# A decoder layer on one core: first norm folded into the second, router by eight-largest, convolution as matmuls, new order on every engine

## The reference, cut to what matters

```python
x = layernorm(x + mamba(x))              # no learned scale, eps 1e-5
x = layernorm(x + retention(x, ctx))     # q from x, k and v from ctx
x = layernorm(x + moe(x))

# mamba: inner width 256, 16 states
x_b, z = split(x @ W_in)
xc    = silu(conv_b + sum_k shift(x_b, 3 - k) * conv_w[:, k])      # 4 taps, causal
delta = softplus((xc @ W_x)[:, :8] @ W_dt + b_dt);  B, C = (xc @ W_x)[:, 8:24], [:, 24:40]
h_t   = exp(delta * A) * h_{t-1} + delta * B * xc                   # 256 channels x 16 states
y     = (sum_s h * C + D * xc) * silu(z);  out = y @ W_out
# retention: q, k rotated; ((q k^T) * decay_mask) v, no softmax: linear in q
# moe: logits = x @ W_r + bias; top 2 of 16 experts (first index on ties), softmax of the two;
#      sum of the chosen experts down(silu(gate) * up), plus one shared expert
```

## Time and profile before

| | |
|---|---|
| time, median of three | 1213.99 us |
| the profiled execution: its own time, its span | 1216.39 us, 1214.6 us |
| first scan starts, last scan ends | 31.05 us, about 1137.6 us |
| busy in the span: VectorE, TensorE, ScalarE, GpSimd | 1093.3, 1080.0, 997.8, 989.8 us |
| ScalarE table loads | 163, 1283 ns each |
| TensorE's granted clock, mean | 0.967 |

### The profile page before, as it was taken

The page is one execution under the profiler, slowest core; times in us unless marked ns, Lnnn a source line. Parts: engine busy times, 40 slices in busy tenths (PEclk is TensorE's granted clock), DMA queues, the critical chain, the costliest instruction groups (busy, mean ns, idle before and its releaser), DMA issues.

```text
span 1214.6 us, 18948 instructions
## 1 busy us (share of the span) xinstructions
PE 1080.0 (89%) x6049; PEld 766.0 (63%) x6049; DVE 1093.3 (90%) x1598; ACT 997.8 (82%) x2288; POOL 989.8 (81%) x623
## 2 busy tenths in 40 slices
PE   5677888989999898999989898998989899988897
PEld 2455666666666766666666666666666667666565
DVE  2899999999999999999999999999999999999523
ACT  5677888989888898988889898988889898888343
POOL 0587797979988897998888799888979888898844
PEclk9687999999999999999999999999999999999999
DMA  6344454545464454546455444645444465454221
GB/s 181 141 164 154 142 174 150 187 141 182 158 202 158 159 183 143 188 150 209 150 169 173 159 173 153 206 160 173 159 172 161 157 204 165 159 179 158 70 80 58
DMA packets 84116, 194.55 MB, mean 160 GB/s; under 512 B 17288, under 2 KB 47936, under 8 KB 67632
## 3 DMA queue, kind: packets, MB, share of 16 engines
q1 hardware_dynamic: 84016, 193.33, 47.3%
HBM read 179.14 MB, written 5.77 MB: 152 GB/s over the span
## 4 chain that ended last, share of the span: by engine, by line
ACT 34%; DVE 26%; PE 24%; issue 11%; POOL 3%; DMA 0%; SPq 0%; DVEq 0%; POOLq 0%; ACTq 0%
ACT decay L680 15%; PE bank L283 14%; DVE state L822 14%; DVE drive_bank L720 6%; PE y_bank L287 6%; ACT L680 4%; ACT silu L656 2%; PE down_bank L283 2%; PE bank L287 2%; ACT L636 1%; ACT L648 1%; ACT L656 1%; POOL hid L916 1%; ACT x_rows L526 1%; POOL read L873 1%
## 5 line engine op out<-in xcount | busy, mean ns | idle before, releaser
L873 POOL TENSOR_TENSOR read<-state,bc_all 128x1024 f32<-128x1024 f32 x256 | 605.4, 2365 | 162.4 <-DVE state L822 139.0
L822 DVE TENSOR_TENSOR_SCAN state<-decay,drive_bank 128x512 f32<-128x512 f32 x512 | 593.9, 1200 | 0.0
L680 ACT ACTIVATE decay<-delta,a_neg 128x252 f32<-128x252 f32 x1024 | 420.4, 494 | 0.8
L720 DVE TENSOR_TENSOR drive_bank<-dx_bank,bc_all 128x512 f32<-128x512 f32 x512 | 327.3, 685 | 0.3 <-DVE state L822 0.3
L287 PE MATMUL y_bank<-ident,read 128*128 128x128 f32 x2048 | 285.7, 287 | 40.4 <-POOL read L873 40.3
L287 PEld LDWEIGHTS y_bank<-ident,read 128*128 128x128 f32 x2048 | 246.2, 148 | 90.6 <-POOL read L873 57.6
L916 POOL TENSOR_TENSOR hid<-gu,comb_all 128x512 f32<-128x512 f32 (+1 forms) x136 | 165.0, 1213 | 20.1 <-DVE gu L837 16.6
L283 PE MATMUL down_bank<-down_w,hid 128*128 128x128 f32 x1024 | 140.9, 280 | 15.1 <-POOL hid L916 12.6
L656 ACT ACTIVATE silu<-bank 128x512 f32<-128x512 f32 (+1 forms) x153 | 87.3, 571 | 81.4 <-PE bank L283 79.6
L283 PEld LDWEIGHTS down_bank<-down_w,hid 128*128 128x128 f32 x1024 | 127.0, 191 | 38.0 <-POOL hid L916 28.6
L837 DVE TENSOR_TENSOR gu<-silu,bank 128x512 f32<-128x512 f32 (+1 forms) x136 | 86.8, 638 | 56.7 <-PE bank L283 30.0
(11 more groups left out here) (126 smaller groups left out, 1496.3 us busy)
## 6 DMA issues: line engine op xcount, KB each, us to landing
bc_all<-bc_dram SPq DMA_DIRECT2D x128, 1024.0 KB, 4.9
comb_all<-comb_dram SPq DMA_DIRECT2D x240, 128.0 KB, 4.5
x_in<-in_x_dram SPq DMA_DIRECT2D x15, 256.0 KB, 6.0
ctx_in<-in_ctx_dram SPq DMA_DIRECT2D x15, 256.0 KB, 5.2
k_pair<-k_pair SPq DMA_DIRECT2D x30, 128.0 KB, 2.1
q_pair<-q_pair SPq DMA_DIRECT2D x30, 128.0 KB, 2.0
out_dram<-y_out SPq DMA_DIRECT2D x15, 256.0 KB, 5.6
comb_all<-comb_dram SPq DMA_DIRECT2D x32, 64.0 KB, 2.7
```

The source lines that it names most:

```text
L680: done = e.activation(seqs(decay_t[j % DECAYS][:, i, h, :])[:, :, 1:T], seqs(delta[c % 2][:, h, sub * SUB:(sub + 1) * SUB])[:, :, 1:T], AC ...
L720: e.tensor_tensor(drive_bank[:, n, :, :], dx_bank[:, :, :], bc_all[group % BC_BUFS][:, 0, PAIR * i + n, :].unsqueeze(1).to_broadcast([P, H ...
L822: e.tensor_tensor_scan(one(state_t[j % STATE_BUFS], n), one(decay_t[j % DECAYS], n), one(drive_bank, n), 0.0, ALU.mult, ALU.add).then_inc( ...
L873: e.tensor_tensor(read_t[j % READS][:, :, :, :], state_t[j % STATE_BUFS][:, :, :, :], bc_all[group % BC_BUFS][:, 1, PAIR * i:PAIR * (i + 1 ...
```

## The change

Slots give way to ticks, four to a step, and every stage is placed anew from one table, in ticks after the begin of its chunk, and once more for the last chunk. (The stages of each step keep their relations: drive and scan on VectorE, `read` at the fourth tick, the transposes two steps later.)

```diff
+TICKS, SUM_AFTER = 4, 2
+AT = {
+    "xT_mm": [(-45, -52)],  "tap_mm": [(-42, -40), (-36, -38)],  "proj_mm": [(-34, -28)],
+    "out_mm": [(69, 69)],  "x1T": [(68, 68)],  "r1_var_mm": [(85, 71)],  "r1_var": [(87, 74)],
+    "xc": [(-33, -42), (-31, -31)],  "top_tanh": [(131, 112)],
+    "dx": [(-12, -14), (10, -14)],  "dx_bank": [(-5, -9), (30, -83)],
+    "gate_mm": [
+        (136, 143), (139, 162), (142, 164), (151, 186), (156, 188), (163, 206), (176, 212), (179, 260), (179, 261)],
+    "gu": [
+        (140, 131), (142, 142), (148, 146), (156, 179), (164, 206), (173, 213), (180, 213), (187, 257), (189, 262)],
+    "pick": [(134, 114)],  "weigh": [(134, 120)],
...
+}
+WHOLE_DRIVES = (3, 7)
+WHOLE_SCANS = (3,)
+EXP_AT = [-10, -9, -4, -3, -3, 1, 3, 17, 21, 21, 28, 37, 37, 39, 41, 53]
-        EXP_AT = [10, 27]
-        EXP_SLOTS = 7
-        FFN_AT = [69, 70, 72, 76, 78, 84, 88, 90, 91]
```

```diff
-                if (c := chunk_at(slot, -21, -22)) is not None:
-                    mm(bank.t[:, 0:width(c)], w_in[:, P:2 * P], xT[c % 3][:, 0:width(c)]).then_inc(S["xb_mm"], 1)
+                for c, h in due(tick, "tap_mm"):
                     for n in range(TAPS):
+                        done = mm(seqs(bank.t[:, 0:width(c)])[:, :, n:T], w_tap[:, h, TAPS - 1 - n, :],
                                   seqs(xT[c % 3][:, 0:width(c)])[:, :, 0:T - n], start=n == 0, stop=n == TAPS - 1)
```

```diff
-                        mm(bank.t[:, cols], xT[c % 3][:, cols], center[:, :], stop=False)
-                        for h in range(HALVES):
-                            done = mm(bank.t[:, cols], y_gatedT[:, h, cols], w_out[:, h, :], start=False,
+                    mm(bank.t[:, 0:width(c)], center[:, :], xT[c % 3][:, 0:width(c)], stop=False)
+                    for h in range(HALVES):
+                        done = mm(bank.t[:, 0:width(c)], w_out[:, h, :], y_gatedT[:, h, 0:width(c)], start=False,
-                    square(bank_of["out", c][:, :], x1, LN1, c)
-                    normalise(bank_of["out", c][:, :], x1, LN1, c)
+                    copy(x1T[:, 0:width(c)], bank_of["out", c][:, 0:width(c)]).then_inc(S["x1T"], 1)
+                    e.activation(r1_sq[:, 0:width(c)], bank_of["out", c][:, 0:width(c)], ACT.Square, scale=D ** -0.5)
+                    for q in range(blocks_of(c)):
+                        done = mm(bank.t[:, 2 * q:2 * q + 2], r1_sq[:, q * P:(q + 1) * P], eps_col[:, :])
+                    e.activation(r1_var[:, 0:blocks_of(c)], of_block[:, :, 0], ACT.Copy, bias=LN_EPS * LN_EPS,
+                    e.tensor_tensor(var_eps[i][:, 0:n], squares[i][:, 0:n], r1_var[:, 0:n], ALU.add)
```

```diff
+                    for q in range(n):
+                        done = e.max(top[:, q, :], logits[:, q, :])
+                    e.tensor_tensor(rank[:, 0, 0:n, :], logits[:, 0:n, :], second, ALU.is_equal)
+                    e.tensor_tensor(soft[:, 0, 0:n], top[:, 0:n, 0], top[:, 0:n, 1], ALU.subtract)
+                    e.tensor_tensor(rank[:, 1, 0:n, :], rank[:, 0, 0:n, :], back..., ALU.mult)
+                    e.tensor_tensor(hot[:, 0, 0:n, :], logits[:, 0:n, :], second, ALU.is_gt)
+                    for q in range(n):
+                        done = e.max(top_at[:, q, :], rank[:, 1, q, :])
+                    e.tensor_scalar(soft[:, 4, 0:n], soft[:, 0, 0:n], 0.0, 0.5, ALU.is_equal, ALU.mult)
+                    e.tensor_tensor(hot[:, 1:3, 0:n, :], back..., top_at..., ALU.is_equal)
+                    e.tensor_tensor(weighted[:, :, 0:n, :], hot[:, :, 0:n, :], soft[:, 2:5, 0:n]..., ALU.mult)
+                    e.tensor_reduce(comb..., weighted..., AXIS.X, ALU.add)
+                    e.activation(soft[:, 1, 0:n], soft[:, 0, 0:n], ACT.Tanh, scale=0.5)          # ScalarE
+                    e.activation(soft[:, 2, 0:n], soft[:, 1, 0:n], ACT.Copy, bias=0.5, scale=0.5)
+                    e.activation(soft[:, 3, 0:n], soft[:, 1, 0:n], ACT.Copy, bias=0.5, scale=-0.5)
```

```diff
+                step = (j + SUB_STEPS) % (SUBS * SUB_STEPS)
+                if 0 <= j < STEPS and part < (1 if step in WHOLE_DRIVES else PAIR):
+                    a, b = (0, PAIR) if step in WHOLE_DRIVES else (part, part + 1)
+                if 0 <= j < STEPS and PAIR <= part < PAIR + (1 if step in WHOLE_SCANS else PAIR):
```

More of the change, by code:

```diff
@@ L236, in half_at @@
[L236 to L248, removed]
@@ new lines, in decoder_layer @@
+        DUE = {name: {} for name in AT}
+        for name, places in AT.items():
+            for n, (normal, last) in enumerate(places):
+                due_of(name, n, normal, last)
+        EXP_DUE = {}
+        for j in range(STEPS):
+            half, n = divmod(j, SUB_STEPS)
+            virtual, sub = divmod(half + 1, SUBS)
+            step = SUB_STEPS * sub + n
+            place = SUB_TICKS * (SUBS * virtual - 1) + (EXP_AT[step] if virtual < CHUNKS - 1 else LAST_EXP_AT[step])
+            EXP_DUE.setdefault(place, []).append(j)
@@ L277, in take @@
                     w.wait_ge(*bank.free)
-                bank.slot = slot + until
+                bank.slot = tick + until
                 bank_of[key] = bank.t
@@ L356, in _ @@
                     bank.free = (S["flip_copy"], 3)
-                if (c := chunk_at(slot, 31, 9)) is not None:
-                    bank = take(("ctxT", c), slot, 1)
+                for c in due(tick, "ctxT_mm"):
+                    bank = take(("ctxT", c), tick, 2)
                     w.wait_ge(S[f"ctx_load{c % 2}"], 16 * (c // 2 + 1))
@@ L364, in _ @@
                     bank.free = (S["ctxT"], at(c))
-                if (c := chunk_at(slot, 35, 35)) is not None:
-                    bank = take(("k", c), slot, 1)
+                for c in due(tick, "k_mm"):
+                    bank = take(("k", c), tick, 2)
                     w.wait_ge(S["ctxT"], at(c))
@@ L370, in _ @@
                     bank.free = (S["k_copy"], at(c))
-                if (c := chunk_at(slot, 36, 35)) is not None:
-                    bank = take(("v", c), slot, 1)
+                for c in due(tick, "v_mm"):
+                    bank = take(("v", c), tick, 2)
                     w.wait_ge(S["ctxT"], at(c))
@@ L413, in _ @@
+                for c in due(tick, "q_mm"):
+                    bank = take(("q", c), tick, 2)
                     w.wait_ge(S["x1T"], at(c))
@@ L425, in _ @@
                     bank.free = (S["ret_copy"], at(c))
-                if (c := chunk_at(slot, 54, 47)) is not None:
-                    bank = take(("retout", c), slot, 4.5)
+                for c in due(tick, "retout_mm"):
+                    bank = take(("retout", c), tick, 9)
                     w.wait_ge(S["ret"], at(c))
@@ L443, in _ @@
                     bank.free = (S["x2T"], at(c))
-                if (c := chunk_at(slot, 63, 56)) is not None:
-                    bank = take(("router", c), slot, 1.5)
+                for c in due(tick, "router_mm"):
+                    bank = take(("router", c), tick, 3)
                     w.wait_ge(S["x2T"], at(c))
@@ L643, in _ @@
-                for part, where in enumerate((4, 21, 17)):
-                    if (half := half_at(slot, where, part)) is not None:
-                        c, sub = half
-                        w.wait_ge(S["z_mm"], subs_before(c) + sub + 1)
-                        w.wait_ge(S["y_gated"], subs_before(c))
-                        e.activation(gate_z[:, sub, :, :].rearrange("p q n -> p (q n)"), bank_of["z", c, sub][:, :],
-                                     ACT.Silu, scale=1.0).then_inc(S["gate_z"], 1)
@@ L650, in _ @@
-                for index, (where, last) in enumerate(zip(FFN_AT, LAST_FFN_AT)):
-                    if (c := chunk_at(slot, where, last)) is None:
-                        continue
+                for c, sub in due(tick, "gate_z"):
+                    w.wait_ge(S["z_mm"], subs_before(c) + sub + 1)
+                    w.wait_ge(S["y_gated"], subs_before(c))
+                    e.activation(gate_z[:, sub, :, :].rearrange("p q n -> p (q n)"), bank_of["z", c, sub][:, :],
+                                 ACT.Silu, scale=1.0).then_inc(S["gate_z"], 1)
@@ L653, in _ @@
+                for c, index in due(tick, "silu"):
                     total = TILES * c + index
```

642 lines of the change are left out of this document (331 added, 311 removed).

## The result

The kernel after takes 1198.69 us (median of four runs, 1194.01 to 1204.63), beside 1214.42 for the kernel before in the same comparison (four runs, 1212.94 to 1217.0). The ratio is 0.987, with an interval of 0.982 to 0.992: faster by some 16 us (1.3%, which is clear of the noise but small), where 46 were forecast. The time is inside the range given, but only a third of the gain came.

The account below looks back on a forecast made before the run. VectorE was taken to bound the kernel, with TensorE leading after the change. A period 2.7 us shorter over 15.7 periods gave -42.4, with the tail -46.4: about 1168 us, range 1132 to 1204.

Parts of the forecast that it names:

- What bounds the kernel before: Whole period of 70.41 us: VectorE has no slack, so what leaves its stream shortens the period until another engine is as long.
- VectorE's work: VectorE's stream per period: 68.0 us less 2.1 for convolution and 1.1 for router, giving 64.8.
- TensorE's work: TensorE's queue per period: 63.1 us now, 65.6 after taps, projection, transposes and variance matmuls; it ties with VectorE and leads.
- Whole drives and scans: VectorE's drives and scans, same columns in three fewer instructions: no gain, ends -0.2 and +0.2 us.
- Table loads: ScalarE's function tables: 163 loads before, 183 after, one more a period at +1.28 us.
- the third rival: ScalarE: Tanh has a table set of its own, two more loads a period (2.6 us), 1196 us; chance 0.06.
- Head and tail: Before and after the repeating middle: head zero (-4 to +5 us), tail -4 us (-10 to +6).
- What is late next is TensorE's queue: After the change: TensorE's in-order queue holds the step's transposes behind bank waits; `read`, then the scan, wait behind them.
- The forecast of 67.7: Period after: TensorE's 65.6 us plus VectorE's present waits of 2.1, which is -2.7 a period; chance 0.61.
- My other sum: Period by VectorE alone: its 64.8 us of work plus 2.4, giving 67.2.
- The second rival: VectorE alone counts: TensorE fits in, `silu` waits go, period 65.2 us, 1124 us in all; chance 0.20.
- The first rival: TensorE keeps its waits, with a second convolution half holding a PSUM bank: period 72.95 us, 1250 us; chance 0.09.

Follow-up runs that it names:

- the places mended: Kernel after with k's rotation, q's swap, the B and C store, last-chunk k swap and two comb_all loads re-placed: 1160.44 us, ratio 0.955.
- one part alone: Kernel before with only the new router (`MAX8`, one block, `Tanh`) in the old router's slots: 1190.01 us, ratio 0.978.

## Why the prediction was wrong

Right, by its own steps:

- *What bounds the kernel before.* VectorE's stream. The router alone, 2.0 us off this stream, took 1.8 off the period.
- *VectorE's work.* 64.8 forecast, from 68.0. Busy time fell by 3.4 a period, and the two parts give more, 4.1 (63.9 left): no row of the convolution is left, and the router went from 4.8 to 2.8, not 3.7. Below is its block in the timeline of after (540.91 - 538.10 = 2.81). The two groups of four `MAX8` take 0.43 and 0.32 from start to start of what follows, 0.75 for eight, where I took 1.4 by the nearest row: this term was 0.7 too large.

```profile
538.10 0.22 DVE L814 TENSOR_TENSOR logits<-bank,router_bias 128x64 f32<-128x64 f32 x1
538.36 0.41 DVE L818 MAX8 top<-logits 128x8 f32<-128x16 f32 x4
538.79 0.22 DVE L821 TENSOR_TENSOR rank<-logits,top 128x64 f32<-128x64 f32 x1
...
539.33 0.40 DVE L829 MAX8 top_at<-rank 128x8 f32<-128x16 f32 x4
539.65 0.15 DVE L832 TENSOR_SCALAR soft<-soft 128x4 f32<-128x4 f32 x1
...
540.91 1.21 DVE L773 TENSOR_TENSOR_SCAN state<-decay,drive_bank 128x512 f32<-128x512 f32 x1
```

- *TensorE's work.* 65.6 forecast; busy 66.7 measured in after, and 652.89 / 9.92 = 65.8 with the places mended. Busy time counts an end ahead of each pause, as the prediction said: the named pauses fell from 95 in ten periods to 43 in 9.86 and 28 in 9.92. The 68.2 of busy time, were all of them kept, did not come. The variance matmuls cost 0.95 (0.96 forecast), the output projection 541.54 - 538.87 = 2.7 (2.6 forecast, 2.8 before):

```profile
538.87 1.02 PE L355 MATMUL bank<-xT,center 128*128 128x512 f32 x2
539.73 1.97 PE L355 MATMUL bank<-y_gatedT,w_out 128*128 128x512 f32 x4
541.54 0.60 PE L364 MATMUL bank<-ident,comb 128*16 128x128 f32 x4
...
555.01 0.95 PE L355 MATMUL bank<-eps_col,r_sq 128*128 128x2 f32 x8
```

- *Whole drives and scans.* Nothing: a drive of 1024 columns takes 1.23 us and two of 512 take 1.27; the scans 2.28 and 2.32.
- *Table loads, and the third rival.* 179 loads (183 forecast; 217 would have been the rival). ScalarE's timeline shows `Tanh` (L718) between exponentials with no load at either side. The Trainium skill (ScalarE: Activation LUTs, "Table sets: the hidden batching unit") lists tanh in the set of exp, and the trace agrees:

```profile
328.10 1.71 ACT L732 ACTIVATE decay<-delta,a_neg 128x252 f32<-128x252 f32 x4
...
330.83 0.20 ACT L718 ACTIVATE soft<-soft 128x4 f32<-128x4 f32 x1
...
331.27 1.67 ACT L732 ACTIVATE decay<-delta,a_neg 128x252 f32<-128x252 f32 x4
```

- *Head and tail.* First scan at 29.73 us (31.05 before): -1.3, forecast 0. Last scan ends at 1131.8, so the tail is 70.8 (77 before): -6, forecast -4. With 4.6 less between them that is the span's 12.0.

Wrong: *"GpSimd loses two tiny instructions of this norm; at 61.5 busy it is not what ends a wait, and I count nothing"*, and with it *"What is late next is TensorE's queue"*. Both judged an engine by its load. GpSimd's load did not grow (60.5 a period, 61.5 before); what changed is what its queue waits for, and where. 6.2 us a period were new waits for the two swaps, `read` stood behind them, and the scan behind `read`. I had said that GpSimd holds `read` with two buffers, and had walked TensorE's and ScalarE's new order, but never SyncE's, where the swap of q went behind a load of 1 MB, and never set the tick of a transfer (87) beside that of its consumer (86). That step cost 70.07 - 67.46 = 2.6 us a period, which mending three places gave back; the whole gain forecast was 2.7, and 0.34 had come. The prediction's own sign of being wrong was a period above 69.5, "which would mean that the new waits, not the work, set it": it is 70.07, and so it was. That the time of 1198.69 lies near the third rival's 1196 and inside the range is luck: its table loads did not come.

The forecast of 67.7 would then be met, but for a part of its reason that fell. I had TensorE lead and VectorE wait 2.1 on top. With the places mended, VectorE is nearer to the bound: 64.1 of work and 3.1 of waits. 2.44 us more on it costs 1.39 a period; 1.7 less on TensorE, at one place of its queue, gives 0.39. My other sum, by VectorE's work and its waits, had given 67.2 and was the sounder one. The second rival (VectorE alone, period 65.2) failed at its waits: none for `silu` is left in after, as it said, but others took their place.

The first rival, slower with TensorE keeping its waits (period 72.95, 1250 us), is close to what the new convolution does in the old places (73.16, 1252). TensorE did keep them there: 67.5 busy and 5.7 idle. The rival gave the banks as the reason; of this the trace shows 1.1 us a period (`xc` waits, 9.9 us in nine periods, where it was 2.4 in ten), and beside it the order in TensorE's queue, which the rival did not name. In the kernel after, with the new places, no wait for `xc` at a bank is among TensorE's waits, so it did not decide the change.

What stays open: what holds the mended version at 67.46. A loop from scan over `read`, TensorE's sums and `y_gated` back to VectorE has a wait of about 2 us at each `y_gated`; two moves inside it changed nothing, and extra work on VectorE takes up little of it (0.3). The first norm and the new places for ScalarE and TensorE were not run alone, so their share is known from the rows above only.

## What to carry to other kernels

When a change gives every stage a new place, the work saved is only half of the sum. Write down for each transfer which instruction needs it, how far behind it that one stands, and what is ahead of it in the issuing queue; a consumer at the same place as its transfer holds everything behind it on its engine. An engine that is not the busiest can still set the period if the busiest one's buffers come back through its queue: look at what its queue waits for, not at its load. And try the parts in the old places first: here one part alone gave as much as the whole, likely more.

## What the runs showed of the hardware that was not expected

- The same swap of 128 KB landed in 2.0 us in the kernel before (2.1 with all places mended, 3.0 with q's swap alone moved), and in 5.3 in after, where it is issued 0.8 us behind the load of 1 MB (which itself takes 5.2) and one of `ctx`.
- One `MAX8` of 16 columns has a record of 0.16 us, and four in a row take 0.41: 0.08 more for each further one. A `TENSOR_TENSOR` of 64 columns takes 0.22 in the same block.
- Eight matmuls of 2 columns take 0.95 us, eight of 16 columns 0.96: at these widths the columns made no difference.
